# Dividing the attention sums head by head on ScalarE, a group ahead

## The chip, the cores and the metric

One core of one Trainium2 chip runs the whole program in one launch. The metric is the device time of the program in microseconds (us); lower is better.

## What is computed

A graph network layer on 12,500 nodes of 256 features and 200,000 edges in float32: a normalised input goes through graph attention with four heads of 64 features and through linear attention; both are added to the residual; a mixture of eight experts (two for each node) follows. The change lies where the sums over a node's edges are divided by the softmax denominators and go on into the rest of the layer:

```python
alpha = ex / (denom[dst] + 1e-16)
msg = h[src] * alpha[..., None]
out = jax.ops.segment_sum(msg, dst, num_segments=n)
return out.reshape(n, H * F) + bias
...
y = h + x
mu = jnp.mean(y, axis=-1, keepdims=True)
var = jnp.mean((y - mu) ** 2, axis=-1, keepdims=True)
y = (y - mu) / jnp.sqrt(var + 1e-05) * ln_gamma + ln_beta
return jax.nn.relu(y)
...
x = x + _L0_gnn_ref(...) + _L0_mix_ref(...)
x = x + _L0_ffn_ref(_layernorm(x), ...)
```

The kernel sums `ex * h` and `ex` for each node and head over the edges, and divides afterwards: one factor `1 / denom` for each node and head, times 64 features.

## The kernel before, in words

The program has stages with a barrier of all engines between them: `project` (node features), planning, `attend_edges` (the pass over the edges, until about 2281 us of the trace), `finish` (until the experts start) and `run_experts`. The edge pass leaves its sums in SBUF, in `s.big` seen as `s.sums[128, 98, 264]`: 98 tiles of 128 nodes, for each node 256 sums and four denominators.

`finish` (L1465) takes the tiles in 14 groups of 7 (`CHUNKS`, `CHUNK`). Each engine has its own program, and they meet in semaphores that count groups or tiles. `c` is a group.

- **SyncE** loads three tables of 896 KB for each group, `xn` (residual), `hh` (mixed) and `x_row` (x), into buffers for two groups. `load(c)` waits until group c-2 is joined (`joined`); it is issued behind `store(c-2)`, which writes that group's result, 896 KB, to `out`. Behind the loads of group 12 it waits for the store of group 10 and then issues the experts' weights.
- **VectorE** takes the groups in a written order (the loop over `n` at its end): `divide(n)`, `gat_scale(n)`, `join(n-1)`, `choose(n-2)`, `ffn_square(n-1)`, `take_slots(n-2)`, `ffn_scale(n-1)`, `tag(n-2)`. `divide` (L1816) multiplies the seven tiles by `rden` (L1818), waits for the loads, adds `xn` (L1821, counted by `summed`), takes statistics (L1824) and the moments, and asks for a root (`root_in`). `rden` is one reciprocal over all denominators (L1950), ahead of group 0. `gat_scale` makes the layer norm's scale and bias from the root. `join` (L1837) does five passes over seven tiles (L1840 to L1849), the last counted by `joined`, then statistics (L1852) and moments, and asks for the first root of the next norm (L1861). `choose` picks the experts. `ffn_square` (from L1866) and `ffn_scale` (to L1881) turn two roots into that norm's scale.
- **ScalarE** runs `in_turn` over five steps: `gat_root(c)` (L1695), `scale_tiles(c)` (L1707 and L1708, seven of each: the gain, and the tile scaled in place), then `ffn_roots(c-1)` (L1714, two), `odds_of(c-2)` (L1718), `make_rows(c-1)` (L1729 and L1733, seven of each). A square root and an exponential lie in different tables, so it loads one (ACT_TABLE_LOAD) in each direction once a group.
- **TensorE** transposes the rows and computes the router's logits; **GpSimd** scatters each finished group's rows to the experts' regions, 14 indirect DMAs for each group (L1686).

In VectorE's setup the order is: the reciprocal, `divide(0)`, `gat_scale(0)`, a few constants, and then the loop with `divide(1)` ahead of `join(0)`.

Of the kernel before, what the change touches and what calls it, by code (L numbers as in the profile page):

```python
# [11 lines left out]
P = 128  # L12
N = 12500
D = 256
# [4 lines left out]
GH = 4  # L19
GF = D // GH  # L20
# [3 lines left out]
SUM = D + GH  # L24
# [26 lines left out]
CHUNK = 7  # L51
CHUNKS = TILES // CHUNK
# [26 lines left out]
ALU = mybir.AluOpType  # L79
ACT = mybir.ActivationFunctionType  # L80
# [102 lines left out]
def in_turn(steps, lag, count):  # L183

    for n in range(count + max(lag)):
        for k, step in enumerate(steps):
            if 0 <= n - lag[k] < count:
                step(n - lag[k])
# [1276 lines left out]
def finish(nc, s, x, ln_gamma, ln_beta, w_norm2, gamma, beta, Wr, br, W1, b1, W2, out):  # L1465


    with ExitStack() as ctx:
# [6 lines left out]
        def sem(name):  # L1475
            return nc.alloc_semaphore(name=name)
# [17 lines left out]
        rden = s.shift[:, :, 0:GH]  # L1494
# [57 lines left out]
        mix_rooted = sem("f_mix_rooted")  # L1552
        a_mix_ready = sem("f_a_mix_ready")
        root_in = sem("f_root_in")
        rooted = sem("f_rooted")
        summed = sem("f_summed")
        gat_scales = sem("f_gat_scales")
# [26 lines left out]
        def part(c):  # L1584
            return slice(c * CHUNK, (c + 1) * CHUNK)

        def tiles(c):
            return s.sums[:, part(c), 0:D]
# [4 lines left out]
        def scatters(j, groups):  # L1593
            return 16 * 2 * CHUNK * len(range(j, groups, ROW_RING))

        with nc.Block() as block:
# [93 lines left out]

            @block.scalar
            def _(act):
                def gat_root(c):
                    act.wait_ge(root_in, c + 1)
                    act.activation(gat[:, c % 2, 2, :], gat[:, c % 2, 2, :], ACT.Sqrt).then_inc(rooted, 1)  # L1695

                def scale_tiles(c):
                    u = c % 2
                    act.wait_ge(gat_scales, 2 * (c + 1))
                    if c >= 2:  # L1700
                        act.wait_ge(joined, c - 1)
                    if c == 0:
                        act.wait_ge(a_mix_ready, 1)
                        act.wait_ge(w_in, 16 * W_LOADS)
                    for i in range(CHUNK):
                        t = c * CHUNK + i
                        act.activation(gain[:, u, i, :], w2_b[:, :], ACT.Identity, bias=s.ones[:, 0:1], scale=a_mix[:, t:t + 1]).then_inc(gained, 1)  # L1707
                        act.activation(s.sums[:, t, 0:D], s.sums[:, t, 0:D], ACT.Identity,  # L1708
                                       bias=gat[:, u, 4, i:i + 1], scale=gat[:, u, 3, i:i + 1]).then_inc(normal, 1)

                def ffn_roots(c):
                    for k in range(2):
                        act.wait_ge(ffn_root_in, 2 * c + k + 1)
                        act.activation(ffn[:, c % 2, 2, :], ffn[:, c % 2, 2, :], ACT.Sqrt).then_inc(ffn_rooted, 1)  # L1714

                def odds_of(c):
                    act.wait_ge(gap_ready, c + 1)
                    act.activation(odds[:, c % 2, :], gap[:, c % 2, :], ACT.Exp).then_inc(odds_ready, 1)  # L1718

                def make_rows(c):  # L1720
                    u = c % 2
                    j = c % ROW_RING
                    act.wait_ge(ffn_scales, 2 * (c + 1))
                    if c >= ROW_RING:
                        act.wait_ge(scattered[j], scatters(j, c))
                    for i in range(CHUNK + 1):
                        t = c * CHUNK + i
                        if i < CHUNK:
                            act.activation(rows[:, j, i, 0:D], s.sums[:, t, 0:D], ACT.Identity,  # L1729
                                           bias=ffn[:, u, 5, i:i + 1], scale=ffn[:, u, 4, i:i + 1]).then_inc(rows_ready, 1)  # L1730
                        if i >= 1:
                            act.wait_ge(rowsT_psum, t)
                            act.activation(rowsT[:, (t - 1) % 2, :, :], ps_t[:, (t - 1) % 2, 0:D].rearrange("p (c n) -> p c n", c=C), ACT.Copy).then_inc(rowsT_ready, 1)  # L1733

                act.wait_ge(mix_root_in, 1)
                act.activation(a_mix[:, :], a_mix[:, :], ACT.Sqrt).then_inc(mix_rooted, 1)
                in_turn([gat_root, scale_tiles, ffn_roots, odds_of, make_rows], [0, 0, 1, 2, 1], CHUNKS)

            @block.tensor
            def _(pe):  # L1740
# [49 lines left out]
            def _(v):  # L1790
                done = [0]

                def then(ins):
                    done[0] += 1
                    ins.then_inc(chain, 1)

                def settle():
                    v.wait_ge(chain, done[0])
# [7 lines left out]
                def moments_of(st, twice_mean, var, tmp):  # L1806
                    then(v.tensor_tensor(twice_mean, st[:, :, 1], st[:, :, 4], ALU.add))
                    then(v.tensor_tensor(tmp, st[:, :, 1], st[:, :, 4], ALU.subtract))
                    then(v.tensor_tensor(var, st[:, :, 2], st[:, :, 5], ALU.add))
                    settle()  # L1810
                    then(v.scalar_tensor_tensor(tmp, tmp, 0.25, tmp, ALU.mult, ALU.mult))
                    settle()
                    then(v.scalar_tensor_tensor(var, var, 1.0 / D, tmp, ALU.mult, ALU.add))
                    settle()

                def divide(c):  # L1816
                    heads = tiles(c).rearrange("p t (h f) -> p t h f", h=GH)
                    then(v.tensor_tensor(heads, heads, rden[:, part(c), :].unsqueeze(3).to_broadcast([P, CHUNK, GH, GF]), ALU.mult))  # L1818
                    settle()
                    v.wait_ge(loaded[c % 2], 48 * (c // 2 + 1))  # L1820
                    v.tensor_tensor(tiles(c), tiles(c), xn[:, c % 2, :, :], ALU.add).then_inc(summed, 1)  # L1821
                    v.wait_ge(summed, c + 1)
                    for i in range(CHUNK):
                        then(v.bn_stats(stats[:, c % 2, i, :], s.sums[:, c * CHUNK + i, 0:D]))  # L1824
                    settle()
                    g = gat[:, c % 2, :, :]
                    moments_of(stats[:, c % 2, :, :], g[:, 0, :], g[:, 1, :], g[:, 2, :])
                    v.tensor_scalar(g[:, 2, :], g[:, 1, :], 1e-5, None, ALU.add).then_inc(root_in, 1)
# [118 lines left out]

                mean_and_variance(v, s.mix_stats, mix_mean[:, :], a_mix[:, :], mix_tmp[:, :], mix_agg)
                then(v.tensor_tensor(mix_tmp[:, :], mix_mean[:, :], mix_mean[:, :], ALU.mult))
                then(v.reciprocal(rden[:, :, :], s.sums[:, :, D:SUM]))  # L1950
                settle()
                v.scalar_tensor_tensor(a_mix[:, :], a_mix[:, :], 1e-6, mix_tmp[:, :], ALU.add, ALU.add).then_inc(mix_root_in, 1)
                divide(0)
                v.wait_ge(mix_rooted, 1)
                v.reciprocal(a_mix[:, :], a_mix[:, :]).then_inc(a_mix_ready, 1)
# [21 lines left out]
                for n in range(CHUNKS + 2):  # L1977
                    if n == CHUNKS + 1:
                        scale_weights()
                    if 1 <= n < CHUNKS:  # L1980
                        divide(n)
                        gat_scale(n)
                    if 1 <= n <= CHUNKS:
                        join(n - 1)
                    if n >= 2:
                        choose(n - 2)
                    if 1 <= n <= CHUNKS:
                        ffn_square(n - 1)
                    if n >= 2:
                        take_slots(n - 2)  # L1990
                    if 1 <= n <= CHUNKS:
                        ffn_scale(n - 1)
                    if n >= 2:
                        tag(n - 2)
# [233 lines left out]
def program(nc, x, src_table, dst_row, dst_table, dst, W, att_src, att_dst, gat_bias, ln_gamma, ln_beta, w_norm1, w_qkv, w_out, b_out, w_norm2,  # L2228
            gamma, beta, Wr, br, W1, b1, W2, b2, out):
    with ExitStack() as ctx:  # L2230
# [37 lines left out]
        with stage(nc):  # L2268
            s.experts_in = nc.alloc_semaphore(name="x_experts_in")
            finish(nc, s, x, ln_gamma, ln_beta, w_norm2, gamma, beta, Wr, br, W1, b1, W2, out)  # L2270
            run_experts(nc, s, b2, out)
# [34 lines left out]
```

## Time and profile before

| | |
|---|---|
| median of 3 runs | 3586.68 us (3580.91 to 3588.13) |
| the profiled execution, its own time | 3580.47 us |
| its span from the first to the last instruction | 3578.8 us |
| TensorE, VectorE, ScalarE, GpSimd busy, share of the span | 78%, 66%, 36%, 60% |
| granted TensorE clock over the span | 0.901 |

The page's head gives the span and each engine's busy time. Lines of a timeline read: start, duration (both us), engine, line of the kernel, operation, output<-inputs, shapes, count, and in brackets how long the engine had stood idle before it and what ended that. SPq and POOLq are the engines that issue DMAs. A list of waits gives who waited for what, the total in us, how often, and the longest.

### The profile page before, as it was taken

To read this page: it belongs to the slowest core of one execution; us is meant where nothing else is said; L and a number is where in the kernel's file an instruction comes from. 1 tells how busy PE (TensorE), PEld (TensorE's weight loads), DVE (VectorE), ACT (ScalarE), POOL (GpSimd) and SP (SyncE) were. 2 spreads that over 40 slices of the span, in tenths; PEclk is the share of its full clock that TensorE was granted. 3 is DMA by queue.
4 is the path that set the end of the run, shared out by engine and by line. 5 is a ranking of instruction groups with operands and counts; after the bars stand their busy time and mean duration, and the time that the engine had idled before them with its cause. 6 is when DMAs were issued, how large, how long until landed. Compare 5 with 4: busy or idle time off the path is not lost. (4 is left out here: it accounts for less than half of the span.)

```text
span 3578.8 us, 70224 instructions
## 1 busy us (share of the span) xinstructions
PE 2793.4 (78%) x17326; PEld 2290.8 (64%) x17327; DVE 2344.6 (66%) x6486; ACT 1288.4 (36%) x4257; POOL 2154.1 (60%) x2117
## 2 busy tenths in 40 slices
PE   6757788888888888888888888433335799999997
PEld 4535666666666666666666666323335799999997
DVE  6655666666566667777777777888878455555554
ACT  5723333333333333333333333355542233333332
POOL 3167777777776777776666666246656344444443
PEclk9979999999999999999999999755555899999999
DMA  7656666666665667666666666445582344444443
GB/s 246 238 133 155 159 159 155 160 158 161 158 157 147 155 158 191 184 184 179 179 175 176 171 170 169 134 153 175 182 277 101 74 71 71 71 71 71 71 71 52
DMA packets 384652, 529.69 MB, mean 148 GB/s; under 512 B 64276, under 2 KB 323559, under 8 KB 384218
## 3 DMA queue, kind: packets, MB, share of 16 engines
q0 software_dynamic: 114496, 265.49, 32.3%
q1 hardware_dynamic: 185112, 183.84, 18.2%
q10 hardware_dynamic: 84770, 77.19, 6.8%
q8 instruction: 112, 1.84, 0.2%
q14 instruction: 162, 1.33, 0.1%
HBM read 394.80 MB, written 132.72 MB: 147 GB/s over the span
## 5 line engine op out<-in xcount | busy, mean ns | idle before, releaser
L1119 POOL DMA_INDIRECT rows<-node_rows,index x1552 | 1475.7, 951 | 581.3 <-issue 446.5
L1397 PE MATMUL ps_sum<-msg,hot 128*128 128x260 f32 x3904 | 1021.7, 407 | 18.0 <-DVE big L1216 1.7
L1397 PEld LDWEIGHTS ps_sum<-msg,hot 128*128 128x128 f32 x3904 | 730.7, 197 | 134.2 <-issue 5.2
L2126 POOL DMA_INDIRECT out_dram<-big x204 | 353.3, 1732 | 437.8 <-DVE big L2218 388.7
L1199 DVE TENSOR_TENSOR msg<-rows,ps_w 128x1024 f32<-128x1024 f32 x488 | 596.2, 1222 | 16.9 <-issue 2.6
L1377 PE MATMUL ps_hot<-ident_h,hotT 128*128 128x128 bf16 x1952 | 194.5, 223 | 300.7 <-DVE hotT L1175 298.7
L2177 ACT ACTIVATE x_actT<-x_ps_hT,b1T 128x128 f32<-128x128 f32 x816 | 233.2, 369 | 523.0 <-PE x_ps_hT L2152 522.9
L1284 ACT ACTIVATE e<-e 128x16 f32<-128x16 f32 x488 | 105.3, 216 | 878.1 <-DVE e L1193 865.1
L2152 PEld LDWEIGHTS x_ps_hT<-x_rowsT,x_w_now 128*128 128x128 f32 x3264 | 398.1, 192 | 11.5 <-DVE x_w_now L2196 1.1
L1686 POOL DMA_INDIRECT expert_in<-f_rows,f_slot x196 | 260.4, 1329 | 231.6 <-ACT f_rows L1729 174.6
L2152 PE MATMUL x_ps_hT<-x_rowsT,x_w_now 128*128 128x128 f32 x3264 | 399.1, 276 | 0.7 <-DVE x_w_now L2196 0.7
L1377 PEld LDWEIGHTS ps_hot<-ident_h,hotT 128*128 128x128 bf16 x1952 | 128.5, 99 | 404.6 <-DVE hotT L1175 397.4
L2161 PE MATMUL x_ps_out<-big,x_actT 128*128 x1632 | 386.0, 379 | 0.3 <-ACT x_actT L2177 0.3
L1279 ACT ACTIVATE hot<-ps_hot 128x512 f32<-128x512 bf16 x488 | 286.0, 586 | 246.1 <-PE ps_hot L1377 241.8
L2161 PEld LDWEIGHTS x_ps_out<-big,x_actT 128*128 128x128 f32 x1632 | 294.2, 190 | 32.2 <-issue 0.6
L1224 DVE SCALAR_TENSOR_TENSOR area<-ps_kv,area 128x256 f32<-128x256 f32 x98 | 41.6, 425 | 325.7 <-ACT area L1313 325.7
L2191 DVE COPY x_rowsT<-x_ps_t 128x256 f32<-128x256 f32 x204 | 86.7, 425 | 250.0 <-PE x_ps_t L2142 250.0
L1175 DVE TENSOR_SCALAR hotT<-targets,pair_node_id 128x512 bf16 x488 | 181.0, 371 | 95.1 <-SPq L1081 94.4
L1216 DVE TENSOR_TENSOR big<-big,ps_sum 128x260 f32 x488 | 202.8, 415 | 3.7 <-PE ps_sum L1397 2.1
L1409 PE MATMUL ps_kv<-wq,area 128*128 128x512 f32 x392 | 185.5, 596 | 0.0
L2218 DVE SCALAR_TENSOR_TENSOR big<-x_ps_out,x_weight,x_bias 128x256 f32<-128x256 f32 x204 | 98.8, 484 | 122.2 <-issue 115.9
L1746 PE MATMUL f_ps_rank<-f_taken,f_earlier 128*128 128x56 f32 x28 | 9.4, 440 | 215.5 <-DVE f_taken L1908 215.5
(289 smaller groups left out, 4163.2 us busy)
## 6 DMA issues: line engine op xcount, KB each, us to landing
targets<-dst_row SPq DMA_DIRECT2D x391, 128.0 KB
big<-expert_in SPq DMA_DIRECT2D x204, 130.0 KB, 2.1
rows<-node_rows,index POOLq DMA_INDIRECT x1564
node_rows<-big SPq DMA_DIRECT2D x14, 924.0 KB
turned<-rT SPq DMA_DIRECT2D x14, 896.0 KB, 4.5
area<-turned ACTq DMA_DIRECT2D x98, 128.0 KB
queries<-area ACTq DMA_DIRECT2D x98, 128.0 KB
area<-queries ACTq DMA_DIRECT2D x98, 128.0 KB
```

Source lines behind the costliest of these rows:

```text
L1119: g.indirect_dma_start(rows[:, j, k, :], None, s.node_rows, bass.IndirectOffsetOnAxis(ap=index[:, b, j * G + k:j * G + k + 1], axis=0)).th ...
L1199: v.tensor_tensor(m[:, :, 0:D].rearrange("p g (h f) -> p g h f", h=GH), rows[:, bass.ds(here, 1), :, 0:D].rearrange("p j g (h f) -> p (j g ...
L1216: v.tensor_tensor(dest, dest, ps_sum[:, j % 2, 0:SUM], ALU.add).then_inc(sum_added, 1)
L1279: act.activation(hot[:, j % MSGS, :], ps_hot[:, 0:SPAN], ACT.Copy).then_inc(hot_ready, 1)
L1377: mm = pe.transpose(ps_hot[:, k * P:(k + 1) * P], hotT[:, j % 2, k * P:(k + 1) * P], ident_h[:, :])
L1397: mm = pe.matmul(ps_sum[:, j % 2, 0:SUM], hot[:, j % MSGS, k * P:(k + 1) * P], msg[:, j % MSGS, k, :], start=(k == 0), stop=(k == G - 1))
L1409: pe.matmul(ps_kv[:, :], rT[:, u, c * P:(c + 1) * P], s.wq[:, c, D:3 * D], start=(c == 0), stop=(c == C - 1))
L1686: g.indirect_dma_start(s.expert_in, bass.IndirectOffsetOnAxis(ap=slot[0:count, j, k, i:i + 1], axis=0), rows[0:count, j, i, :], None).then ...
L2126: g.indirect_dma_start(out, bass.IndirectOffsetOnAxis(ap=rows[:, j, D:D + 1].bitcast(I32), axis=0), outs[:, j, :], None, compute_op=ALU.ad ...
L2152: mm = pe.matmul(ps_hT[:, j % 2, k * P:(k + 1) * P], w1_now[:, j % 2, a:a + P], rowsT[:, j % 2, c, :], start=(c == 0), stop=(c == C - 1))
L2161: mm = pe.matmul(ps_out[:, j % 2, 0:D], actT[:, j % 2, c, :], s.w2[:, bass.ds(e, 1), c * D:(c + 1) * D].rearrange("p e n -> p (e n)"), sta ...
L2177: ins = act.activation(actT[:, j % 2, c, :], ps_hT[:, j % 2, c * P:(c + 1) * P], ACT.Gelu, bias=s.b1T[:, bass.ds(e * HC + c, 1)])
```

## The change

The multiplication by `rden` leaves VectorE. ScalarE does it in place, one activation (Copy with the head's factor as scale) for each tile and head, 28 for each group. It divides group 0 as soon as the reciprocal is there, ahead of its root for the mix, and group c+1 directly behind `scale_tiles(c)`, ahead of `ffn_roots(c-1)`. VectorE's `divide(c)` waits until all heads of its group are counted (`divided`) and then goes on with the wait for the loads and the addition. The reciprocal gets a semaphore of its own (`rden_ready`).

```diff
--- before.py
+++ after.py
@@ -1552,6 +1552,8 @@
         mix_rooted = sem("f_mix_rooted")
         a_mix_ready = sem("f_a_mix_ready")
         root_in = sem("f_root_in")
+        rden_ready = sem("f_rden_ready")
+        divided = sem("f_divided")
         rooted = sem("f_rooted")
         summed = sem("f_summed")
         gat_scales = sem("f_gat_scales")
@@ -1690,6 +1692,13 @@
 
             @block.scalar
             def _(act):
+                def divide_heads(c):
+                    act.wait_ge(rden_ready, 1)
+                    for t in range(c * CHUNK, (c + 1) * CHUNK):
+                        for h in range(GH):
+                            head = s.sums[:, t, h * GF:(h + 1) * GF]
+                            act.activation(head, head, ACT.Copy, scale=rden[:, t, h:h + 1]).then_inc(divided, 1)
+
                 def gat_root(c):
                     act.wait_ge(root_in, c + 1)
                     act.activation(gat[:, c % 2, 2, :], gat[:, c % 2, 2, :], ACT.Sqrt).then_inc(rooted, 1)
@@ -1732,9 +1741,15 @@
                             act.wait_ge(rowsT_psum, t)
                             act.activation(rowsT[:, (t - 1) % 2, :, :], ps_t[:, (t - 1) % 2, 0:D].rearrange("p (c n) -> p c n", c=C), ACT.Copy).then_inc(rowsT_ready, 1)
 
+                divide_heads(0)
                 act.wait_ge(mix_root_in, 1)
                 act.activation(a_mix[:, :], a_mix[:, :], ACT.Sqrt).then_inc(mix_rooted, 1)
-                in_turn([gat_root, scale_tiles, ffn_roots, odds_of, make_rows], [0, 0, 1, 2, 1], CHUNKS)
+
+                def divide_next(c):
+                    if c + 1 < CHUNKS:
+                        divide_heads(c + 1)
+
+                in_turn([gat_root, scale_tiles, divide_next, ffn_roots, odds_of, make_rows], [0, 0, 0, 1, 2, 1], CHUNKS)
 
             @block.tensor
             def _(pe):
@@ -1814,9 +1829,7 @@
                     settle()
 
                 def divide(c):
-                    heads = tiles(c).rearrange("p t (h f) -> p t h f", h=GH)
-                    then(v.tensor_tensor(heads, heads, rden[:, part(c), :].unsqueeze(3).to_broadcast([P, CHUNK, GH, GF]), ALU.mult))
-                    settle()
+                    v.wait_ge(divided, (c + 1) * CHUNK * GH)
                     v.wait_ge(loaded[c % 2], 48 * (c // 2 + 1))
                     v.tensor_tensor(tiles(c), tiles(c), xn[:, c % 2, :, :], ALU.add).then_inc(summed, 1)
                     v.wait_ge(summed, c + 1)
@@ -1947,7 +1960,7 @@
 
                 mean_and_variance(v, s.mix_stats, mix_mean[:, :], a_mix[:, :], mix_tmp[:, :], mix_agg)
                 then(v.tensor_tensor(mix_tmp[:, :], mix_mean[:, :], mix_mean[:, :], ALU.mult))
-                then(v.reciprocal(rden[:, :, :], s.sums[:, :, D:SUM]))
+                v.reciprocal(rden[:, :, :], s.sums[:, :, D:SUM]).then_inc(rden_ready, 1)
                 settle()
                 v.scalar_tensor_tensor(a_mix[:, :], a_mix[:, :], 1e-6, mix_tmp[:, :], ALU.add, ALU.add).then_inc(mix_root_in, 1)
                 divide(0)
```

On ScalarE, at the head of `finish` up to the first root of group 1 (`f_a_mix` is the mix's scale, `f_xn` takes the gain, `big` holds the sums, `f_gat` the layer norm's scales). Before:

```order
L1691 UNCONDITIONAL_BRANCH
L1736 ACT_TABLE_LOAD
L1736 ACTIVATE f_a_mix<-f_a_mix 128x98
L1695 ACTIVATE f_gat<-f_gat 128x7
L1707 ACTIVATE f_xn<-f_w_b,ones,f_a_mix 128x256
...
L1708 ACTIVATE big<-big,f_gat 128x256
L1695 ACTIVATE f_gat<-f_gat 128x7
```

Of the change:

```order
L1693 UNCONDITIONAL_BRANCH
L1700 ACTIVATE big<-big,shift 128x64 x28
L1746 ACT_TABLE_LOAD
L1746 ACTIVATE f_a_mix<-f_a_mix 128x98
L1704 ACTIVATE f_gat<-f_gat 128x7
L1716 ACTIVATE f_xn<-f_w_b,ones,f_a_mix 128x256
...
L1717 ACTIVATE big<-big,f_gat 128x256
L1700 ACTIVATE big<-big,shift 128x64 x28
L1704 ACTIVATE f_gat<-f_gat 128x7
```

Group 0's 28 heads now stand ahead of the table load and the mix's root (`shift` is the tensor that holds `rden`), and group 1's stand behind the fourteen activations that scale group 0. In later groups the 28 stand at the same place, ahead of the two roots of `ffn_roots`.

On VectorE, behind the constants of the setup, where the loop begins with group 1. Before:

```order
L1963 TENSOR_TENSOR f_br_b<-f_br_b,f_ps_fold 128x8
L1965 COPY f_running<-f_region 128x8
L1966 MEMSET f_onward 128x64
L1968 MEMSET f_onward 128x8
L1818 TENSOR_TENSOR big<-big,shift 128x7x256
L1821 TENSOR_TENSOR big<-big,f_xn 128x7x256
L1824 BN_STATS f_stats<-big 128x6 x7
```

Of the change:

```order
L1976 TENSOR_TENSOR f_br_b<-f_br_b,f_ps_fold 128x8
L1978 COPY f_running<-f_region 128x8
L1979 MEMSET f_onward 128x64
L1981 MEMSET f_onward 128x8
L1834 TENSOR_TENSOR big<-big,f_xn 128x7x256
L1837 BN_STATS f_stats<-big 128x6 x7
```

The pass over the seven tiles is gone, and the addition (now L1834) follows the constants directly, with its wait for the heads. The rest of VectorE's order is as it was.

## Rows read from the trace of the kernel before

**Rows 1.** The page's head: span, and busy time of each engine.

```profile
span 3578.8 us, 70224 instructions
PE 2793.4 (78%) x17326; PEld 2290.8 (64%) x17327; DVE 2344.6 (66%) x6486; ACT 1288.4 (36%) x4257; POOL 2154.1 (60%) x2117
```

**Rows 2.** The list of waits, 2290 to 2720 us.

```profile
...
POOL expert_in L1686 <- ACT f_rows L1729: 169.4, 12, 77.9
...
DVE big L1821 <- DMA f_x_row<-in_x_dram: 36.5, 13, 7.6
...
```

**Rows 3.** The timeline, all engines, one steady group (2568 to 2600 us).

```profile
...
2568.13 0.38 SPq L1617 DMA_DIRECT2D out_dram<-big  x1
...
2571.60 0.21 ACT L1714 ACTIVATE f_ffn<-f_ffn 128x7 f32<-128x7 f32 x1 [6.40 <-DVE f_ffn L1861]
...
2574.93 0.19 DVE L1866 RECIPROCAL f_ffn<-f_ffn 128x7 f32<-128x7 f32 x1
...
2578.56 0.17 DVE L1881 SCALAR_TENSOR_TENSOR f_ffn<-f_ffn 128x7 f32<-128x7 f32 x1
...
2579.45 2.02 DVE L1818 TENSOR_TENSOR big<-big,shift 128x1792 f32<-128x1792 f32 x1
...
2583.61 2.02 DVE L1821 TENSOR_TENSOR big<-big,f_xn 128x1792 f32<-128x1792 f32 x1 [2.15 <-DMA f_x_row<-in_x_dram]
...
2587.27 1.28 ACT L1695 ACT_TABLE_LOAD   x1
...
2589.07 0.21 ACT L1695 ACTIVATE f_gat<-f_gat 128x7 f32<-128x7 f32 x1 [0.52 <-DVE f_gat L1828]
...
2589.74 0.60 ACT L1707 ACTIVATE f_xn<-f_w_b,ones,f_a_mix 128x256 f32<-128x256 f32 x1 [0.47 <-DVE f_gat L1835]
...
2596.15 0.58 ACT L1708 ACTIVATE big<-big,f_gat 128x256 f32<-128x256 f32 x1
...
2599.66 0.38 SPq L1617 DMA_DIRECT2D out_dram<-big  x1
...
```

**Rows 4.** The timeline, SyncE and VectorE, groups 1 to 3.

```profile
...
2349.27 0.38 SPq L1617 DMA_DIRECT2D out_dram<-big  x1
...
2362.62 2.03 DVE L1821 TENSOR_TENSOR big<-big,f_xn 128x1792 f32<-128x1792 f32 x1
...
2380.26 0.38 SPq L1617 DMA_DIRECT2D out_dram<-big  x1
...
```

**Rows 5.** The timeline, VectorE and ScalarE, the start of `finish`.

```profile
...
2283.70 2.59 DVE L1950 RECIPROCAL shift<-big 128x392 f32<-128x392 f32 x1
...
2292.37 2.02 DVE L1821 TENSOR_TENSOR big<-big,f_xn 128x1792 f32<-128x1792 f32 x1 [3.85 <-DMA f_x_row<-in_x_dram]
...
2300.85 2.01 DVE L1818 TENSOR_TENSOR big<-big,shift 128x1792 f32<-128x1792 f32 x1
...
2304.04 2.02 DVE L1821 TENSOR_TENSOR big<-big,f_xn 128x1792 f32<-128x1792 f32 x1 [1.18 <-DMA f_x_row<-in_x_dram]
...
2305.15 0.59 ACT L1708 ACTIVATE big<-big,f_gat 128x256 f32<-128x256 f32 x1
...
```

**Rows 6.** ScalarE's groups of instructions by line and form, whole span.

```profile
...
L1279 ACT ACTIVATE hot<-ps_hot 128x512 f32<-128x512 bf16 x488 | 286.0, 586 | 246.1 <-PE ps_hot L1377 241.8 <-issue 3.5
...
L2177 ACT ACTIVATE x_actT<-x_ps_hT,b1T 128x128 f32<-128x128 f32 x816 | 233.2, 369 | 523.0 <-PE x_ps_hT L2152 522.9
...
L1708 ACT ACTIVATE big<-big,f_gat 128x256 f32<-128x256 f32 x98 | 57.3, 585 | 0.0
...
L1733 ACT ACTIVATE f_rowsT<-f_ps_t 128x256 f32<-128x256 f32 x98 | 37.5, 382 | 33.4 <-PE f_ps_t L1759 33.4
...
```

**Rows 7.** The timeline, ScalarE, in the experts' stage.

```profile
...
2999.69 1.14 ACT L2177 ACTIVATE x_actT<-x_ps_hT,b1T 128x128 f32<-128x128 f32 x4 [2.59 <-PE x_ps_hT L2152]
...
```

**Rows 8.** The timeline, GpSimd, the first scatters of the steady group.

```profile
...
2580.44 1.90 POOL L1686 DMA_INDIRECT expert_in<-f_rows,f_slot  x1 [7.50 <-ACT f_rows L1729]
2582.64 0.97 POOL L1686 DMA_INDIRECT expert_in<-f_rows,f_slot  x1 [0.30 <-issue]
...
```

## Prediction

> **What bounds the kernel now.** The page's head [rows 1] gives one execution of 3578.8 us and no engine busy all the time, so the stage the change touches has to be read for itself. It is `finish`, from about 2281 us to 2760 us, fourteen groups of seven tiles. The list of waits inside it [rows 2] says who is starved: VectorE stood idle 36.5 us in thirteen places, each before the residual addition (L1821), each time for the last of a group's three loads, and GpSimd stood idle 169.4 us in twelve places. VectorE does the pass that is to go (L1818), so the first question is what its idle time says about the pace.
>
> I followed one steady group on all engines [rows 3] and looked for closed loops. Call J the end of a join, which is where SyncE issues the store (2568.13) and behind it the loads of the group after next. Those land and release the addition at 2583.61, 15.48 us later. From the addition, VectorE's own work leads to the next J at 2599.66, another 16.05 us. Together that is a **load loop** of 31.53 us. In it L1818 (2579.45, 2.02 us) isn't a member: it ran while the loads were in flight, and VectorE waited 2.15 us more after it.
>
> The second loop is **ScalarE's**: J to the last scale of the layer norm before the experts (L1881, 2578.56) 10.43 us; from there ScalarE makes the rows and loads a table, until 2587.27 + 1.28 = 2588.55, 9.99 us; then the root (L1695, 2589.07) to the next J, 10.59 us. Sum 31.01 us. The stores at 2380.26 [rows 4] and 2599.66 [rows 3] are seven groups apart: 219.40 / 7 = 31.34 us each. So the stage runs at the pace of the load loop, and ScalarE's loop is a floor 0.33 us beneath it. One group shows the floor bare: there the addition at 2362.62 waited for no load, and the step between the stores around it (2349.27 to 2380.26) was still 30.99 us [rows 4].
>
> **The change part by part.** *Removed: fourteen passes of 2.02 us on VectorE*, 28.3 us. In the steady groups the landing time depends on J, not on this pass, so the wait of 2.15 us becomes one of about 4.2 us and the next J stays where it is: worth zero. In group 3, with no wait, up to 2.0 us of addition come free, but the root behind it waited for ScalarE anyway; zero again. In group 0 the load lands at 2292.37, 3.85 us after the pass [rows 5]: zero. The ceiling of what the pass can give is the distance to the floor, 0.33 us in about nine groups, 3 us.
>
> *Added: 28 activations per group on ScalarE.* No row has this form (128x64, SBUF to SBUF, a pointer for the scale). From [rows 6]: the copies of 128x512 and 128x256 from PSUM take 586 and 382 ns, so 0.797 ns an element; the in-place scaling of 128x256 with two pointer operands takes 585, so a pointer costs (585 - 382) / 2 = 101 ns. One head: 382 - 192 x 0.797 + 101 = 330 ns. In a row they overlap: from 2589.74 to 2596.15 [rows 3] are 13 steps of 0.493 us for operations of 0.585 us, 0.092 us of overlap. So one every 0.238 us, and a group's heads take 27 x 0.238 + 0.33 = **6.8 us**. Lower bound: four activations of 128x128 with one pointer take 1.14 us [rows 7], one of them 0.369 [rows 6], so 0.257 us apart, less 64 x 0.797 ns is 0.206 us, 5.9 us a group. Upper bound: no overlap, 28 x 0.33 = 9.2 us. I take 0.238, since its rows are SBUF operations behind each other on this very tensor.
>
> *Where they stand in a steady group.* ScalarE's last scaling starts at 2596.15, so heads run from 2596.64 to 2603.4. The root for the experts' layer norm is asked for 3.47 us after J (2571.60 against 2568.13), that is at 2603.13: 0.3 us late. VectorE takes its result only 6.80 us after J (2574.93), behind `choose`, so at 2606.46. The root needs 0.2 us and its way, so heads may end at 2606.2. Cover remains up to a spacing of (2606.2 - 2596.64 - 0.33) / 27 = 0.342 us. Cost: zero, and the same at the upper bound. The heads of group c+1 are complete 20 us before VectorE asks for them.
>
> *Where they stand at the start.* Here nothing covers them. The reciprocal that they need ends at 2283.70 + 2.59 = 2286.29 [rows 5]. Heads of group 0 end at 2286.33 + 6.8 = 2293.1; the load had released the addition at 2292.37: **+0.7 us**. The square root for the mix and its table load stand behind them on ScalarE, some 1.6 us, and are wanted only behind the statistics of group 0, 4 us later: nothing. Then ScalarE scales group 0 and only after that divides group 1. The last scaling starts at 2305.15, now 2305.85, the heads follow at 2306.34 and end at 2313.1. VectorE is through with its constants at 2300.9 and stands before the addition of group 1, which began at 2304.04 when its load had landed. It now begins at 2313.15: **+9.1 us**, the 0.7 included. Behind it on VectorE is the join of group 0, whose signal lets SyncE issue the loads of group 2, so both loops carry the 9.1 us on to the end; no step of them has a clock of its own. Bounds: at 0.206 us the first addition isn't late and the second is at 2311.6, +7.5; without overlap +3.2 and then 2318.1, +14.1.
>
> *Freed on GpSimd.* Of its scatters, the one that began during L1818 took 1.90 us, the next, with VectorE waiting, 0.97 [rows 8]. GpSimd waits for the next group 7.50 us anyway, so the 0.93 us saved in each group come to nothing in the sum. By the Trainium skill's page "SBUF — State Buffer" (its part on the engine and AXI sides) a GpSimd operation and a VectorE one with two SBUF inputs can exclude each other from a shared port for a whole instruction, while a compute operation can't slow a DMA. The trace agrees with the first half; by it GpSimd gains about 13 us over fourteen groups, by the rows none of it is on a loop.
>
> **Sum.** +9.1 us at the start, 0 in the steady groups. Against the profiled execution (3580.5 us) that is 3589.6. The median shown, 3586.7, is 6.2 above that execution; the four executions together average 3584.0, and from there I forecast **3593 us**, 0.25% slower.
>
> **Rivals.** *The delay is swallowed* (within 0.2%). Group 13 waits 7.6 us for its load [rows 2], the longest wait, since the experts' weights pass through SyncE's queue ahead of it. If their time didn't depend on J, 7.6 of the 9.1 us would vanish there: 3585.5. Against it, SyncE issues them only once the store of group 10 has landed, which is late as well. The low spacing with the whole 3 us to the floor comes out alike, 7.5 - 3 = +4.5, 3588.5.
>
> *The landing comes forward* (faster). If the loads in flight were held up by scatters that L1818 delays, or by the pass itself, its removal would shorten J to landing by about its own 2.02 us. In twelve groups that is 24 us, less 9.1: 3569. It decides once a landing comes more than 0.8 us earlier per group and ScalarE's loop shortens with it. Against it stands that loop, 31.01 us, untouched by the change. The Trainium skill's page "SBUF — State Buffer" names such a mechanism for scatters and denies it for plain loads.
>
> *ScalarE becomes the bound* (far slower). It decides from 0.342 us a head. At 585 - 153 = 432 ns and no overlap, 12.1 us a group: the start costs 6.1 and 13.7 us more, the root comes 2.5 us late, ScalarE's loop becomes 33.5 against 31.34, in eleven groups 24 us: +44, 3628. Only a cost of issue or of semaphores absent from [rows 3] would do that.
>
> **How the numbers follow.** Forecast 0.60, delay swallowed 0.27, landing forward 0.08, ScalarE bound 0.05. A measurement tells some 0.2%, 7.2 us, from no change. The forecast's own range, +7.5 to +10.5 on a level uncertain by 3.5 us, lies just above that bound, and an eighth of its chance falls beneath: slower 0.53 + 0.05 = 0.58, same 0.27 + 0.07 = 0.34, faster 0.08. The range is 3583 to 3603: the forecast's, the upper bound of +14 and most of the swallowed case; left out are the two far rivals and some tails.
>
> **What would show it.** L1818's line is gone; 392 activations of 128x64 at about 0.33 us appear; VectorE's idle time before the addition rises from 36.5 by some 38 us, of which 11 stand at group 1 and 3 at group 0, where it waits for ScalarE, the rest for loads; stores stay 31.3 us apart; the roots in the steady groups wait less than 1 us on ScalarE instead of 6.40. It's wrong if stores stand closer than 31.0 us, if the second addition begins less than 7 us later after the stage's start, or if VectorE waits for a root in the steady groups.

## The result

Over twenty runs each, the changed kernel takes 3595.23 us (3584.77 to 3600.11) and the kernel before 3586.64 us (3580.91 to 3595.54). The ratio is 1.0022, with a 95% interval of 1.0014 to 1.0030: **8 us slower**, about what was forecast. The profiled execution took 3596.94 us. The page's head, to be held against [rows 1]:

```profile
span 3595.3 us, 70602 instructions
...
PE 2807.7 (78%) x17326; PEld 2301.1 (64%) x17327; DVE 2318.6 (64%) x6472; ACT 1380.9 (38%) x4649; POOL 2146.4 (60%) x2117
```

VectorE works 26.0 us less (2344.6 to 2318.6), ScalarE 92.5 us more (1288.4 to 1380.9), and the program takes longer. This span is 16.5 us above that of [rows 1], more than the change costs, since this execution reached the stage 6.7 us later: the reciprocal of the denominators begins at 2290.41 and not at 2283.70. So the stage is measured from the end of that reciprocal to VectorE's cast of the final counts (`f_end_row`), here 2770.88 - 2293.00 = 477.9 us, in the kernel before 2754.20 - 2286.29 = 467.9. The stage is **10.0 us** longer. The two ends of the stage, VectorE's timeline, the kernel before first and then the change:

```profile
...
2754.20 0.15 DVE L1996 CAST f_end_row<-f_running 1x8 int32<-1x8 f32 x1
...
```

```profile
...
2770.88 0.15 DVE L2009 CAST f_end_row<-f_running 1x8 int32<-1x8 f32 x1
...
```

The form that no row of before had, from ScalarE's groups by form in the changed kernel:

```profile
...
L1700 ACT ACTIVATE big<-big,shift 128x64 f32<-128x64 f32 x392 | 94.9, 335 | 10.5 <-DVE shift L1963 10.5
...
```

The 335 ns had been estimated at 330. The list of waits of the changed kernel, 2290 to 2740 us, answers to [rows 2]:

```profile
...
POOL expert_in L1688 <- ACT f_rows L1738: 184.6, 12, 87.1
...
DVE big L1834 <- DMA f_x_row<-in_x_dram: 53.1, 12, 10.7
...
DVE big L1834 <- ACT big L1700: 18.2, 2, 11.5
...
ACT f_ffn L1723 <- DVE f_ffn L1874: 6.4, 1, 6.4
...
```

VectorE's idle time before the addition has gone from 36.5 to 53.1 + 18.2 = 71.3 us: 34.8 us more, against 28.2 us of work taken away. It waits where it used to multiply. In the first two groups the wait now ends with ScalarE (18.2 us), where it ended with a load before (3.85 and 1.18 us). The timeline of the changed kernel at the start of the stage, VectorE and ScalarE:

```profile
...
2290.41 2.59 DVE L1963 RECIPROCAL shift<-big 128x392 f32<-128x392 f32 x1
...
2293.03 6.79 ACT L1700 ACTIVATE big<-big,shift 128x64 f32<-128x64 f32 x28 [10.50 <-DVE shift L1963]
...
2299.85 2.03 DVE L1834 TENSOR_TENSOR big<-big,f_xn 128x1792 f32<-128x1792 f32 x1 [6.74 <-ACT big L1700]
...
2313.12 6.77 ACT L1700 ACTIVATE big<-big,shift 128x64 f32<-128x64 f32 x28
...
2319.93 2.03 DVE L1834 TENSOR_TENSOR big<-big,f_xn 128x1792 f32<-128x1792 f32 x1 [11.51 <-ACT big L1700]
...
```

A group's 28 heads last 6.79 us. Counted from the reciprocal's end, the first addition begins at 6.85 (before: 2292.37 - 2286.29 = 6.08) and the second at 26.93 (before 17.75, [rows 5]): **9.2 us late**, after an idle time of 11.51 us that ScalarE ends. A steady group answers to [rows 3]:

```profile
...
2550.72 2.02 DVE L1862 SCALAR_TENSOR_TENSOR big<-big,f_hh 128x1792 f32<-128x1792 f32 x1
...
2582.63 2.02 DVE L1862 SCALAR_TENSOR_TENSOR big<-big,f_hh 128x1792 f32<-128x1792 f32 x1
...
2595.11 0.17 DVE L1894 SCALAR_TENSOR_TENSOR f_ffn<-f_ffn 128x7 f32<-128x7 f32 x1
...
2599.03 2.03 DVE L1834 TENSOR_TENSOR big<-big,f_xn 128x1792 f32<-128x1792 f32 x1 [2.95 <-DMA f_x_row<-in_x_dram]
...
2603.81 1.28 ACT L1704 ACT_TABLE_LOAD   x1
...
2605.11 0.21 ACT L1704 ACTIVATE f_gat<-f_gat 128x7 f32<-128x7 f32 x1
...
2605.34 0.20 DVE L1846 RECIPROCAL f_gat<-f_gat 128x7 f32<-128x7 f32 x1 [0.89 <-ACT f_gat L1704]
...
2612.68 6.79 ACT L1700 ACTIVATE big<-big,shift 128x64 f32<-128x64 f32 x28
...
2613.65 2.02 DVE L1862 SCALAR_TENSOR_TENSOR big<-big,f_hh 128x1792 f32<-128x1792 f32 x1
...
2619.36 0.20 ACT L1723 ACTIVATE f_ffn<-f_ffn 128x7 f32<-128x7 f32 x1
...
```

The last passes of these joins (L1862) stand 31.91 and 31.02 us apart; the seven steps from 2394.10 to this 2613.65 average 31.36 us, against 31.34 before. In the short step the root is there 0.89 us too late for VectorE (2605.34), because ScalarE's table load ended at 2605.09: the floor of the second loop. The load still comes last for the addition (2.95 us of waiting in place of 2.15). The heads run from 2612.68 to 2619.47 and the root behind them at 2619.36 no longer waits 6.40 us, but not at all.

### The profile page after: what moved, and what is told of

It is laid out like the page before. It is cut to its first block and busy times, and to the rows that moved or that the text cites. A ratio compares the mean times of both kernels' runs of the same rounds, so it can differ in the third digit from the quotient of the medians.

```text
span 3595.3 us, 70602 instructions
## 1 busy us (share of the span) xinstructions
PE 2807.7 (78%) x17326; PEld 2301.1 (64%) x17327; DVE 2318.6 (64%) x6472; ACT 1380.9 (38%) x4649; POOL 2146.4 (60%) x2117
## 3 DMA queue, kind: packets, MB, share of 16 engines
q8 instruction: 112, 1.84, 0.2%
## 5 line engine op out<-in xcount | busy, mean ns | idle before, releaser
L1119 POOL DMA_INDIRECT rows<-node_rows,index x1552 | 1475.3, 951 | 589.5 <-issue 444.1
L1397 PE MATMUL ps_sum<-msg,hot 128*128 128x260 f32 x3904 | 1034.6, 411 | 17.7 <-DVE big L1216 1.8
L1688 POOL DMA_INDIRECT expert_in<-f_rows,f_slot x196 | 254.3, 1297 | 247.7 <-ACT f_rows L1738 189.8
```

Source lines behind the costliest of these rows:

```text
L1119: g.indirect_dma_start(rows[:, j, k, :], None, s.node_rows, bass.IndirectOffsetOnAxis(ap=index[:, b, j * G + k:j * G + k + 1], axis=0)).th ...
L1397: mm = pe.matmul(ps_sum[:, j % 2, 0:SUM], hot[:, j % MSGS, k * P:(k + 1) * P], msg[:, j % MSGS, k, :], start=(k == 0), stop=(k == G - 1))
L1688: g.indirect_dma_start(s.expert_in, bass.IndirectOffsetOnAxis(ap=slot[0:count, j, k, i:i + 1], axis=0), rows[0:count, j, i, :], None).then ...
```

## The experiments

All ratios are to the kernel before, timed beside each kernel. "Stage" is the length defined above, from one profile each; "step" is the mean distance of the joins of groups 2 to 9. A profile reads the stage closer than a median of runs reads the program: the kernel before itself ranged from 3570.54 to 3591.98 us in the 29 runs timed with the first four, while the two kernels that were profiled twice gave stages of 431.0 and 433.0, and of 438.8 and 438.8 us. A difference of a us or two between stages is therefore not read as one here.

| run | ratio (95%) | stage us | step us |
|---|---|---|---|
| before | 1 | 467.9 | 31.34 |
| the change | 1.0022 (1.0014 to 1.0030) | 477.9 | 31.36 |
| no division at all | 0.9997 (0.9983 to 1.0010) | 467.8 | 31.25 |
| groups 0 and 1 on VectorE | 0.9998 (0.9987 to 1.0010) | 466.7 | 31.15 |
| group 1's heads early | 0.9995 (0.9983 to 1.0008) | 468.3 | 31.25 |
| heads in halves | 1.0086 (1.0067 to 1.0104) | 500.6 | 32.74 |
| loads first | 0.9980 (0.9969 to 0.9992) | 463.3 | 31.02 |
| root among the rows | 0.9984 (0.9970 to 0.9997) | 464.3 | 31.06 |
| both, division on VectorE | 0.9946 (0.9929 to 0.9962) | 449.8 | 29.41 |
| both, heads of groups 2 to 13 | 0.9936 (0.9918 to 0.9953) | 443.2 | 28.85 |
| both, heads, weights spread | 0.9907 (0.9888 to 0.9926) | 431.0 | 28.85 |
| both, weights spread, VectorE | 0.9926 (0.9906 to 0.9945) | 438.8 | 29.41 |

**Is the pass worth anything?** From the change, neither heads nor pass:

```diff
-                divide_heads(0)
...
-                in_turn([gat_root, scale_tiles, divide_next, ffn_roots, odds_of, make_rows], [0, 0, 0, 1, 2, 1], CHUNKS)
+                in_turn([gat_root, scale_tiles, ffn_roots, odds_of, make_rows], [0, 0, 1, 2, 1], CHUNKS)
...
-                    v.wait_ge(divided, (c + 1) * CHUNK * GH)
```

> The changed kernel without ScalarE's heads and without VectorE's wait for them: the division by the denominators is left out altogether, so both the old pass and the new heads are gone. Theory (the steady groups run at the pace of the load loop with ScalarE's loop 0.33 us beneath; the pass hides under loads in flight): within 3 us of the kernel before (ratio 0.999 to 1.000), stores still 31.0 to 31.4 us apart, VectorE's wait before the addition about 4 us a group. Rival (the landing comes forward with the pass): 24 us faster than before, stores 29.3 us apart.

The stage is 467.8 us with no division anywhere, 0.1 us off the kernel before. VectorE's idle time (waits of that kernel, 2281 to 2730 us) takes up most of the pass:

```profile
...
DVE big L1832 <- DMA f_x_row<-in_x_dram: 61.1, 14, 10.5
...
```

61.1 us in place of 36.5: 24.6 us of the 28.2. Another 2.2 us went into VectorE's waits for the root (5.1 to 7.3 us in the same lists). So the pass was worth nothing to the stage. The rival in which landings come forward can be read directly. From the start of a join's last pass to the addition that its loads release, groups 4 to 12 took 17.38 us on average in the kernel before and 17.04 here, and 17.09 to 17.15 in the change, the two variants below that start differently and the root among the rows. So the landings came some 0.3 us sooner without the pass on VectorE, less than the 0.8 us from which that rival decides. With one profile of each kernel and single landings that scatter over more than a us, what brings them forward is not shown.

**Where do the 9 us arise?** Two edits, each of which gives the start its cover back. First, groups 0 and 1 on VectorE:

```diff
-                divide_heads(0)
...
-                    if c + 1 < CHUNKS:
+                    if 2 <= c + 1 < CHUNKS:
                         divide_heads(c + 1)
...
-                    v.wait_ge(divided, (c + 1) * CHUNK * GH)
+                    if c < 2:
+                        v.wait_ge(rden_ready, 1)
+                        heads = tiles(c).rearrange("p t (h f) -> p t h f", h=GH)
+                        then(v.tensor_tensor(heads, heads, rden[:, part(c), :].unsqueeze(3).to_broadcast([P, CHUNK, GH, GF]), ALU.mult))
+                        settle()
+                    else:
+                        v.wait_ge(divided, (c - 1) * CHUNK * GH)
```

> Groups 0 and 1 divided by VectorE as in the kernel before, groups 2 to 13 by ScalarE's heads. Theory (all of the 9 us lost lies at the start, where nothing covers the heads): back to the kernel before, ratio to it 0.999 to 1.000, the second addition begins 22.2 us after the first table load of the stage, as before. Rival (the heads cost something in every steady group, or the shift is a matter of the longer ScalarE program): stays 5 to 9 us slower than before.

Second, all heads on ScalarE, but group 1's where it is idle:

```diff
                 divide_heads(0)
+                divide_heads(1)
                 act.wait_ge(mix_root_in, 1)
...
-                    if c + 1 < CHUNKS:
+                    if 2 <= c + 1 < CHUNKS:
                         divide_heads(c + 1)
```

> All fourteen groups on ScalarE, but group 1's heads stand behind group 0's, ahead of the mix's root, and no longer behind the scaling of group 0. Theory: ScalarE is idle there; the heads end 13.6 us after the reciprocal, the first root comes 2 us later than in the kernel before, VectorE's constants end about 2 us later too, and the second addition still begins within 1 us of its load's landing. Within 2 us of the kernel before, 7 to 9 us faster than the change. Rival (the delay of the first addition, 0.7 us and what follows, counts in full and the root's delay passes on): 3 to 5 us slower than before.

Both are back at the kernel before, 466.7 and 468.3 us. In the first the second addition begins 17.46 us after the reciprocal's end (before 17.75). The timeline of the second, VectorE and ScalarE:

```profile
...
2299.08 13.47 ACT L1700 ACTIVATE big<-big,shift 128x64 f32<-128x64 f32 x56 [10.50 <-DVE shift L1964]
...
2305.90 2.02 DVE L1835 TENSOR_TENSOR big<-big,f_xn 128x1792 f32<-128x1792 f32 x1 [6.74 <-ACT big L1700]
...
2314.05 0.19 ACT L1704 ACTIVATE f_gat<-f_gat 128x7 f32<-128x7 f32 x1
...
2317.40 2.03 DVE L1835 TENSOR_TENSOR big<-big,f_xn 128x1792 f32<-128x1792 f32 x1
...
```

Fifty-six heads stand in one row and end at 2312.55. The first root, wanted at about 2311, comes at 2314.05, and still the second addition begins 18.35 us after the reciprocal's end, with no wait in front of it, 0.60 us later than before. There are 392 heads in both kernels; only the place of 28 of them makes 9 us. The twelve later groups of heads, which stand behind the scaling in both variants, cost nothing: the loss lies wholly at the start.

**How much cover do the heads have?** Each head in two halves, 56 activations a group:

```diff
-                        for h in range(GH):
-                            head = s.sums[:, t, h * GF:(h + 1) * GF]
-                            act.activation(head, head, ACT.Copy, scale=rden[:, t, h:h + 1]).then_inc(divided, 1)
+                        for h in range(2 * GH):
+                            half = s.sums[:, t, h * GF // 2:(h + 1) * GF // 2]
+                            act.activation(half, half, ACT.Copy, scale=rden[:, t, h // 2:h // 2 + 1]).then_inc(divided, 1)
...
-                    v.wait_ge(divided, (c + 1) * CHUNK * GH)
+                    v.wait_ge(divided, (c + 1) * CHUNK * GH * 2)
```

> Each head is divided in two activations of 128x32, 56 for each group. By the durations, one every 0.212 us, 11.9 us a group. Theory: the start costs 5.1 us more for each of groups 0 and 1 than the change, and the heads end 2.4 us behind the point up to which VectorE's choosing covers them, so ScalarE's loop becomes about 33.4 us against 31.34: 10 + 22 = 32 us slower than the change, 41 slower than before (ratio about 1.0115), stores about 33.3 us apart. Rival (the wait for loads takes up the lateness in the steady groups too): only the start counts, 10 us slower than the change, stores 31.4 us apart.

```profile
...
L1700 ACT ACTIVATE big<-big,shift 128x32 f32<-128x32 f32 x784 | 167.4, 306 | 10.5 <-DVE shift L1963 10.5
...
```

```profile
...
2525.80 11.96 ACT L1700 ACTIVATE big<-big,shift 128x32 f32<-128x32 f32 x56
...
2526.77 2.03 DVE L1862 SCALAR_TENSOR_TENSOR big<-big,f_hh 128x1792 f32<-128x1792 f32 x1
...
2537.66 0.19 ACT L1723 ACTIVATE f_ffn<-f_ffn 128x7 f32<-128x7 f32 x1
...
2537.89 0.20 DVE L1879 RECIPROCAL f_ffn<-f_ffn 128x7 f32<-128x7 f32 x1 [2.20 <-ACT f_ffn L1723]
...
```

The first fence is this kernel's groups by form, the second its timeline, VectorE and ScalarE. The halves take 11.96 us a group, as worked out (11.9). Now the root (2537.66) comes behind the choosing, and VectorE stands 2.20 us in front of the reciprocal that needs it (2537.89); 2.4 had been expected. The step is 32.74 us and not the expected 33.4 (31.01 + 2.4). The lateness was 0.2 us smaller, and 0.47 us of it fill a wait for TensorE's totals that VectorE had there anyway and that is gone from this kernel's waits: 31.01 + 2.20 - 0.47 = 32.74. In the kernel before it is there (waits, 2290 to 2720 us):

```profile
...
DVE f_running L1914 <- PE f_ps_total L1747: 5.7, 12, 0.5
...
```

The stage is 22.7 us longer than the change's, where 32 had been expected: some 7 us of the difference are the shorter steps, and in front of group 13 the step was 2.6 us shorter than the change's (35.53 against 38.14). The second addition is 10.4 us later than there, 10 expected.

**Two loops, taken apart.** If a load loop at 31.5 and a ScalarE loop at 31.01 both bind, then shortening either must give nearly nothing and both together much. In SyncE's order:

```diff
-                    store(c)
                     if c + 2 < CHUNKS:
                         load(c + 2)
+                    store(c)
```

> The kernel before with one edit: SyncE issues the loads of the group after next ahead of the store of the group just joined, so that 896 KB less stand ahead of them. Theory of two loops: the load loop drops from 31.5 to about 28.9 us, but ScalarE's loop stays at 31.01, so stores stay 31.0 us apart; 3 us in the steady groups and 2.6 in front of groups 2 and 13, about 6 to 8 us faster than before, ratio 0.998. Rival (the load loop alone sets the pace): stores 28.9 us apart, 30 us faster.

In ScalarE's, on top of the variant with groups 0 and 1 on VectorE:

```diff
                     for i in range(CHUNK + 1):
                         t = c * CHUNK + i
+                        if i == 5 and c + 2 < CHUNKS:
+                            gat_root(c + 2)
...
-                in_turn([gat_root, scale_tiles, divide_next, ffn_roots, odds_of, make_rows], [0, 0, 0, 1, 2, 1], CHUNKS)
+                in_turn([first_roots, scale_tiles, divide_next, ffn_roots, odds_of, make_rows], [0, 0, 0, 1, 2, 1], CHUNKS)
```

(`first_roots` is `gat_root` for groups 0 and 1 alone.)

> The variant with groups 0 and 1 divided by VectorE and the rest by ScalarE, and one edit: ScalarE takes the root of group c+2 between the fifth and the sixth row of make_rows(c), no longer behind all seven. That shortens ScalarE's loop by some 3 us and leaves the load loop alone. Theory of two loops: the load loop holds the pace, stores 31.3 to 31.5 us apart, within 2 us of that variant and of the kernel before. Rival (ScalarE's loop alone sets the pace): stores below 29 us apart, 25 us faster.

With loads first, the last passes of the joins of groups 2 and 9 (VectorE's timeline), and then two of the waits (2281 to 2730 us):

```profile
...
2384.91 2.02 DVE L1849 SCALAR_TENSOR_TENSOR big<-big,f_hh 128x1792 f32<-128x1792 f32 x1
...
2602.04 2.02 DVE L1849 SCALAR_TENSOR_TENSOR big<-big,f_hh 128x1792 f32<-128x1792 f32 x1
...
```

```profile
...
DVE f_gat L1833 <- ACT f_gat L1695: 19.6, 13, 1.9
...
DVE big L1821 <- DMA f_x_row<-in_x_dram: 17.1, 4, 8.8
...
```

The same with the root among the rows:

```profile
...
2382.24 2.02 DVE L1873 SCALAR_TENSOR_TENSOR big<-big,f_hh 128x1792 f32<-128x1792 f32 x1
...
2599.67 2.02 DVE L1873 SCALAR_TENSOR_TENSOR big<-big,f_hh 128x1792 f32<-128x1792 f32 x1
...
```

```profile
...
DVE big L1845 <- DMA f_x_row<-in_x_dram: 57.3, 14, 10.0
...
```

Loads first: steps of 31.02 us in every steady group, the floor to 0.01 us. VectorE waits for loads in four places only (groups 0, 1, 2 and 13), and in each steady group 1.9 us for ScalarE's root. Root among the rows: every one of fourteen additions waits for its load (57.3 us in all), and the steps lie between 30.65 and 31.55, 31.06 on average. This is the load loop by itself, in a kernel without the steady groups' pass on VectorE. In the kernel before the seven steps that make up 31.34 are the load loop's too: each of their additions waited for its load, and the next join's last pass began 14.0 us behind it, as it does wherever no root is late. The difference of 0.28 us is that of the landings, which took 17.34 us on average over these seven steps and 17.06 with the root among the rows. The stage is 2.4 us shorter than its base's, of which 1.84 lie in the one step that ScalarE's root had held there (30.99 to 29.15). Its ratio is 6 us (1 to 11) under the kernel before where 2 had been expected; the stage accounts for 3.6. Together, once with the division on VectorE and once with the heads:

> The kernel before, division on VectorE, with both edits, loads ahead of the store and the root among the rows. Theory: both old loops are now under 29 us, and the bound is VectorE's own way round, join to scale 10.43, tag and the dividing pass 2.94, addition to root 5.45, root to join 10.59, together 29.4 us: stores 29.4 us apart, about 22 us faster than before, ratio 0.994. VectorE's wait for loads falls under 1 us a group.

> As the run with both edits, but groups 2 to 13 divided by ScalarE's heads. Theory: now the dividing pass stands on the bounding loop, so taking it away is worth something for the first time: stores 28.9 us apart (the load loop again), 4 to 5 us faster than the run with both edits, about 27 us faster than before, ratio 0.9925. Rival (the pass is worth nothing in any case, or ScalarE with 23 us of work a group is in the way): no faster than the run with both edits.

The last passes of the joins of groups 2 and 9, VectorE's timeline, first with the division on VectorE and then with the heads:

```profile
...
2383.36 2.02 DVE L1855 SCALAR_TENSOR_TENSOR big<-big,f_hh 128x1792 f32<-128x1792 f32 x1
...
2589.20 2.02 DVE L1855 SCALAR_TENSOR_TENSOR big<-big,f_hh 128x1792 f32<-128x1792 f32 x1
...
```

```profile
...
2370.41 2.02 DVE L1873 SCALAR_TENSOR_TENSOR big<-big,f_hh 128x1792 f32<-128x1792 f32 x1
...
2572.37 2.03 DVE L1873 SCALAR_TENSOR_TENSOR big<-big,f_hh 128x1792 f32<-128x1792 f32 x1
...
```

That is 29.41 and 28.85 us a step, against 29.4 and 28.9 expected. **The pass has become worth something**: with both loops out of the way VectorE's own way round is the bound (29.41 us in each of ten steps, no load waited for), and the heads take it down to the next one, the loads. The waits of the kernel with heads, 2281 to 2730 us, show it, and where the next time lies:

```profile
...
DVE big L1845 <- DMA f_x_row<-in_x_dram: 36.3, 13, 13.9
...
```

Of the 36.3 us, 13.9 are group 13's, whose loads stand behind the experts' weights. So the weights' sixteen transfers were spread over turns 2 to 10, between a turn's loads and its store:

```diff
+                def weights_behind(c):
+                    due = [k for k in range(2 * EXPERTS) if ((k + 1) * C * HID - 1) // (CHUNK * ROW) == c - 2]
+                    if not due:
+                        return
+                    sp.wait_ge(stored, 16 * c)
+                    sp.wait_ge(measured, c - 1)
+                    sp.wait_ge(rows_ready, (c - 1) * CHUNK)
+                    for k in due:
...
                     if c + 2 < CHUNKS:
                         load(c + 2)
+                    weights_behind(c)
                     store(c)
-                    if c == FREED + 1:
...
```

> The run with both edits and heads on ScalarE, and one more: the experts' weights are issued piece by piece in turns 2 to 10, each between a turn's loads and its store, as soon as the groups that lay in their place are stored, and no longer all at once behind the store of group 10. Theory: the wait of 13.9 us for group 13's loads was the weights' time in SyncE's queue; the store before the last but one and the last join come 28.9 us apart in place of 41.3, the other stores stay 28.9 us apart since the weights travel while the DMA engines have room: 12 us faster than that run, about 35 us faster than before, ratio 0.990. Rival (the DMA engines have no room): stores 30 us apart, nothing gained.

> The same three edits of the order, but the division stays on VectorE for all groups. Theory: stores 29.4 us apart by VectorE's own way round, 11 us faster than the run with two edits on VectorE, 29 us faster than before, ratio 0.992; the heads on ScalarE are worth 6 to 7 us (0.55 us in each of twelve groups) here, where they are worth nothing in the kernel before.

These two were timed where the kernel before took 4462.31 us, 876 us more, nearly all of it in the pass over the edges (the gathers of the first of the two, L1119, begin between 208.8 and 3118.2 us there, and between 206.8 and 2271.9 us when it was timed again); medians 4423.70 and 4429.32, ratios 0.9929 (0.9900 to 0.9958) and 0.9928 (0.9905 to 0.9952). In microseconds that is 32 for either, the intervals too wide to tell the two apart; their stages were 433.0 and 438.8. So the pair was timed once more:

> The same kernel as the run with spread weights and heads on ScalarE, timed again because the kernel before took 4462 us where that one was timed, 876 us more, nearly all of it ahead of the stage in question. In that profile group 13 waited 0.97 us for its loads and the stage from its reciprocal to the last group's counts took 433.0 us, against 467.9 in the kernel before. Theory: 35 us faster than before here too, ratio 0.990. Rival (part of the gain is given back behind the stage): less than 25 us.

> The same pair's other half, division on VectorE: from the reciprocal to the last group's counts 438.8 us, so 29 us faster than before, ratio 0.992, and 6 us slower than the version with heads on ScalarE.

They took 3547.97 us with heads and 3554.77 without, against 3582.42: **34 and 28 us faster than before**. The intervals of the two ratios overlap, so the difference between them rests on the stage. The waits of the faster one, 2281 to 2730 us:

```profile
...
DVE big L1853 <- DMA f_x_row<-in_x_dram: 24.0, 13, 5.2
...
```

The longest is 5.2 us, at group 2, and group 13 waits 1.16. The heads' share is 7.8 us of stage here (438.8 to 431.0), 5.8 in the first profiles of the same two kernels (438.8 to 433.0) and 6.7 in the pair without spread weights (449.8 to 443.2), where 6 to 7 had been expected. In the same stage without the other edits they are worth 0 and, placed as in the change, cost 10.

## Why the prediction was right

*What bounds the stage.* Two loops, with the pass in neither. Each was shortened alone and then both: 31.02, 31.06 and then 29.41 us a step. Shown. ScalarE's floor of 31.01 was right to 0.01 us. The load loop of 31.53 is one group's; its mean in the kernel before is 31.34, which the prediction took from the stores, and 31.06 in the kernel where it alone sets the pace and VectorE has no pass.

*The pass removed: zero.* Shown by leaving the division out, 467.8 against 467.9 us. The steps went from 31.34 to 31.25, so at group 11 the join came 1.3 us sooner, within the ceiling of 3 us, and the step in front of group 13 took 1 us of that back.

*The heads: 6.8 us a group, 330 ns each.* 6.79 us and 335 ns. The distance between them came out as 0.238 from the pair of scalings in [rows 3]; the lower bound from the activations on PSUM, 0.206, would have missed by 0.9 us a group.

*The start: +0.7 and +9.1 us.* 0.77 and 9.18, shown to be the whole loss by two edits that take it away.

*The steady cover.* 2.8 us to spare were forecast and a limit at 0.342 us a head, 9.6 us a group. With 11.96 us the lateness was 2.20 against 2.4 expected. The mechanism was right; what lateness costs was oversized by the 0.47 us a group that VectorE had waited for TensorE there anyway.

*The delay is carried to the end.* Between group 2 and group 12 the additions came 8.2 to 9.8 us late, as the landings scatter, at group 12 8.8; at group 13, behind the weights, 10.0. The swallowed delay, the rival with the most chance, didn't happen: what the weights wait for came later too. The prediction has no term for the 1.2 us that group 13 adds. The step in front of it was 36.95 us in the kernel before 38.14 in the change, 37.93 with no division at all and 37.40 and 37.23 in the two variants of the start; why is open. The stage ends 10.0 us late, the ratio over twenty runs gives 8 (5 to 11), against 9.1 forecast. The level was forecast at 3584.0 and came out at 3586.64, so the forecast of 3593 for the change lies 2.2 us under the 3595.23 measured.

*Signs.* The rise of VectorE's idle time was 34.8 us where 38 stood. Stores stay 31.4 us apart, and ScalarE no longer stands idle in front of the roots for the experts' norm. VectorE does wait 0.84 to 0.89 us for the other root (L1846) in three steady groups, where 0.28 is usual, which could be taken for the last sign of being wrong. The kernel with no division at all shows the same, 0.70 to 1.00 us in three steady groups: it is ScalarE's floor, in the steps where the load came early enough, and not the heads.

*GpSimd.* The forecast that its freed time lies on no loop holds: 196 scatters ran on average 1297 ns in place of 1329 and 6.1 us less in all, and its idle time between groups rose from 169.4 to 184.6 us. The Trainium skill's page "SBUF — State Buffer" (section "SBUF: two separate sides") says the loser of the shared port waits for the whole instruction. Of the estimate of 13 us, 0.93 us for each of fourteen passes, about half appeared. The two timelines show why. Ten scatters began during the pass alone, with 9.2 us more than ten at 0.97 us each. In the change those that begin beside the addition have 15.1 us more than at 0.97, where they had 12.6 before: part of what was freed is lost again beside the next pass.

## What to carry to other kernels

Idle time in front of the instruction behind yours is the first thing to look at: if the work ends in a wait for something that doesn't depend on it, removing it buys only waiting. Write down every closed loop of a pipeline with its length from one set of rows; the gain of any edit is capped by the distance to the next one, some tenths of a us a step here, and two edits that were worth 4.6 and 2.4 us of the stage apart were worth 18.1 together. Work moved to an idle engine a turn ahead needs a look at the first turns: there is no earlier turn to hide it in, and a delay there runs through every later one.

## What was not expected

Where two of the kernels were timed first, the kernel before took 4462 us, and their profiled runs had a granted clock of 0.82 against 0.90, yet the steps of this stage stayed at 29.0 and 29.41 us. What made the pass over the edges longer there was not looked into. A stage's length between two of its own instructions compares kernels where runs that spread over 20 us can't.

Issuing the loads ahead of the store was worth 2.4 us at group 2 (the step in front fell from 29.19 to 26.76) and 2.2 us a step where it set the pace (31.06 to 28.85), but it gave nothing in front of group 13. By the order of issue, the weights wait for the store of group 10, which now stands behind the loads. From the join of group 10 to that of group 12 took 68.8 us before and 69.2 with loads first.
